# Loading ten tables at once and selecting from four of them unsplit, in a DLRM tower kernel

## The reference

```python
e = jnp.stack([tbl_f[ids[:, f]] for f in range(26)], axis=1)
combined = concatenate([dense[:, None, :], e], axis=1)            # 27 vectors a sample
interactions = einsum('bfd,bgd->bfg', combined, combined)
z = concatenate([dense, interactions[:, iu, ju]], axis=1)         # the 351 pairs
h = concatenate([z, dense], axis=1)
h = maximum(h @ W_top1 + b_top1, 0)                               # 607 -> 512
h = maximum(h @ W_top2 + b_top2, 0)                               # 512 -> 256
y = h @ W_top3                                                    # 256 -> 1
```

## Time and profile before

| | us |
|---|---|
| median of 3 runs | 474.64 |
| lowest and highest | 474.0, 475.17 |
| the profiled execution | 473.68 |
| its span in the profile | 471.9 |
| PE busy in the span | 409.8 (87%) |
| DVE busy | 298.0 (63%) |
| POOL busy | 250.7 (53%) |
| ACT busy | 240.6 (51%) |

### The profile page before, as it was taken

How to read it: one execution, slowest core, us unless ns; L and a number is a source line. 1 busy time by engine, 2 the same in 40 slices (tenths; PEclk the granted TensorE clock), 3 DMA queues, 4 the chain that set the end, 5 groups by cost and what they waited for, 6 DMA issues and landing times.

```text
span 471.9 us, 9190 instructions
## 1 busy us (share of the span) xinstructions
PE 409.8 (87%) x3384; PEld 383.0 (81%) x3384; DVE 298.0 (63%) x925; ACT 240.6 (51%) x558; POOL 250.7 (53%) x263
## 2 busy tenths in 40 slices
PE   1676799987998899998999799999999799888997
PEld 1565698876997799878898698988988699777876
DVE  3799597773556847665566766577665767544341
ACT  2341677562354745375454744466442834459462
POOL 0567355554555665656656556566666556564000
PEclk9979899998899999999999999999999999999999
DMA  7996134214132142223522153222522123111000
GB/s 192 255 264 170 39 72 100 67 35 100 46 71 64 41 102 66 64 57 59 97 63 74 39 81 79 73 64 51 96 72 71 44 71 77 41 43 32 13 1 0
DMA packets 24612, 35.95 MB, mean 76 GB/s; under 512 B 6296, under 2 KB 18720, under 8 KB 24568
## 3 DMA queue, kind: packets, MB, share of 16 engines
q1 hardware_dynamic: 16376, 18.57, 17.6%
q0 software_dynamic: 8192, 16.79, 14.2%
HBM read 35.33 MB, written 0.01 MB: 75 GB/s over the span
## 4 chain that ended last, share of the span: by engine, by line
PE 65%; DVE 9%; issue 7%; DMA 6%; ACT 6%; another core or an unknown queue 4%; SPq 1%; POOL 0%; POOLq 0%; DVEq 0%; ACTq 0%
PE gram_ps L425 18%; PE x_ps L406 14%; PE x_ps L407 12%; DVE hot L888 7%; PE x_ps L387 6%; DMA rows<-in_tbl_dram,ids_sb 5%; PE tail_ps L470 3%; PE tail_ps L468 3%; PE tail_ps L469 3%; ACT x L647 3%; PE tail_ps L460 2%; DVE gram L866 1%; DMA x<-in_tbl_dram 1%; ACT pairs L647 1%
## 5 line engine op out<-in xcount | busy, mean ns | idle before, releaser
L353 POOL DMA_INDIRECT rows<-in_tbl_dram,ids_sb x256 | 250.0, 976 | 186.9 <-PE x_ps L406 49.2
L888 DVE TENSOR_SCALAR hot<-ids_all,row_f 125x256 fp32r<-125x256 int32 x640 | 195.8, 374 | 53.8 <-PE x_ps L407 37.8
L406 PE MATMUL x_ps<-hot,table_hi 125*128 125x256 f32 x640 | 166.9, 297 | 36.4 <-issue 11.9
L406 PEld LDWEIGHTS x_ps<-hot,table_hi 125*128 125x128 f32 x640 | 124.3, 194 | 46.7 <-issue 35.5
L407 PE MATMUL x_ps<-hot,table_lo 125*128 125x256 f32 x640 | 160.5, 286 | 0.2
L407 PEld LDWEIGHTS x_ps<-hot,table_lo 125*128 125x128 f32 x640 | 124.7, 195 | 0.6 <-issue 0.6
L425 PE MATMUL gram_ps<-x 128*108 128x108 f32 x1024 | 109.8, 261 | 4.2 <-issue 3.2
L425 PEld LDWEIGHTS gram_ps<-x 128*108 128x108 f32 x1024 | 104.2, 177 | 5.7 <-issue 3.6
L647 ACT ACTIVATE picked<-x_ps 128x256 f32<-128x256 f32 x80 | 30.5, 382 | 90.4 <-PE x_ps L407 54.1
L866 DVE COPY gram<-gram_ps 44x208 f32<-44x208 f32 (+1 forms) x120 | 44.3, 369 | 32.3 <-remote 20.2
L647 ACT ACTIVATE gram<-gram_ps 44x208 f32<-44x208 f32 (+3 forms) x136 | 45.9, 337 | 32.3 <-remote 13.6
(11 more groups left out here) (74 smaller groups left out, 342.1 us busy)
## 6 DMA issues: line engine op xcount, KB each, us to landing
ids_all<-in_selected_ids_dram SPq DMA_DIRECT2D x80, 128.0 KB
rows<-in_tbl_dram,ids_sb POOLq DMA_INDIRECT x256
x<-in_tbl_dram SPq DMA_DIRECT2D x6, 448.0 KB
stage<-in_tbl_dram SPq DMA_DIRECT2D x3, 448.0 KB
rows<-in_r_dense_features_dram SPq DMA_DIRECT2D x16, 64.0 KB
stage<-in_W_pairs_dram SPq DMA_DIRECT2D x1, 702.0 KB
stage<-in_W_dense_dram SPq DMA_DIRECT2D x2, 256.0 KB
stage<-in_W_dram SPq DMA_DIRECT2D x1, 512.0 KB
```

The lines of the kernel that those rows point to most:

```text
L353: pool.indirect_dma_start(out=rows[t][:, slot, :], out_offset=None, in_=tables[GATHERED[slot - 1]], in_offset=bass.IndirectOffsetOnAxis(ap ...
L406: first = pe.matmul(bank, table_hi[j][:, c, :], v, start=(c == 0), stop=False)
L888: last = dve.tensor_scalar(hot[h][:, c, :], ids_all[0:VK, j % IDS, :], row, None, ALU.is_equal)
```

## The change

All ten raw tables get a home of their own, `raws`, in the very memory of the `table_lo` tensors; a table is split in place. SP loads all ten tables one after the other, with their ids; those of tables 5 to 9 go into new buffers `ids_start` in the memory of `x`. The weights come right behind, without a wait, and then the ids of macro tile 1. `loads_begun` is signalled after table 1.

Tables 2, 4, 6 and 8 (`WHOLE_TABLES`) are selected from as loaded at the start: eight float32 products in place of sixteen float32r ones (`select_whole`). ACT makes their high parts as before; DVE makes their low parts in macro tile 0, between the one-hots of tables 0 and 1 of the next macro tile.

The one-hots of the start go through five buffers in turn (`START_HOTS`), three of them in the memory of `x`; from macro tile 1 on they have two as before. The gathers begun are 24 and 23 in steps 0 and 1 in place of 22 and 22, so from step 1 on three more are ahead, and the first five have no ticks to wait for.

```diff
+    START_HOTS = 5
+    WHOLE_TABLES = [2, 4, 6, 8]
+    SPLIT_ORDER = [j for j in range(NS) if j not in WHOLE_TABLES] + WHOLE_TABLES
+    def hot_place(number):
+        return number % START_HOTS if number < 2 * NS else number % HOTS
-    BEGUN = [22, 22, 34, 34, 34, 34, 34, 34]
-    assert len(BEGUN) == NM and sum(BEGUN) + 8 == NM * GATHERS
+    BEGUN = [24, 23, 34, 34, 34, 34, 34, 34]
+
+    FREE = 4
+    assert len(BEGUN) == NM and sum(BEGUN) + 5 == NM * GATHERS
...
-                return ticks + number * ticks_of(step) // begun
+                free = FREE if step == 0 else 0
+                return ticks + max(number - free, 0) * ticks_of(step) // (begun - free)
...
-                sp.wait_ge(hi_ready, 6)
-                sp.wait_ge(lo_ready, 6)
                 sp.dma_start(w1a_raw, W1_dense[0:D, :]).then_inc(weights_loaded, 16)
...
-            for j in range(RAWS):
+            for j in range(NS):
                 if j < IDS:
                     load_ids_all(0, j)
+                else:
+                    load_ids_start(j)
                 load_table(j)
-            sp.sem_inc(loads_begun, 1)
+                if j == 1:
+                    sp.sem_inc(loads_begun, 1)
             for t in range(TILES):
                 load_dense(0, t)
             load_ids(TILES, B // P, ids_loaded[1])
-            for j in range(IDS, NS):
-                if IDS < j <= IDS + NS - RAWS:
-                    load_table(RAWS + j - IDS - 1)
-                sp.wait_ge(hot_ready, 2 * (j - IDS + 1))
-                load_ids_all(0, j)
             load_weights()
...
+            def select_whole(j):
+
+                pe.wait_ge(raw_loaded[j], 32)
+                bank = x_bank(0, start_use(j))[:].rearrange("p a b -> p (a b)")[:, 0:MACRO]
+                for c in range(VC):
+                    number = hot_number(0, j, c // HALF)
+                    if c % HALF == 0:
+                        pe.wait_ge(hot_ready, number + 1)
+                    last = pe.matmul(bank, table_raw[j][:, c, :], hot_buffers[hot_place(number)][:, c % HALF, :].bitcast(F32),
+                                     start=(c == 0), stop=(c == VC - 1))
+                    if c % 2 == 0:
+                        last.then_inc(paced, 1)
...
             def macro_tile(m, before):
                 transposes(m, 0, 2)
-                if not before:
-
-                    act.wait_ge(lo_ready, NS)
                 join(m, 1, 0)
...
+            def split_table(j):
+                dve.wait_ge(hi_ready, j + 1)
+                if j in WHOLE_TABLES:
+
+                    dve.wait_ge(x_filled, x_before(0, start_use(j) + 1))
+                low_part(table_lo[j][:], table_raw[j], table_hi[j][:]).then_inc(lo_ready, 1)
...
+                if not before:
+                    for j in WHOLE_TABLES:
+                        split_table(j)
                 build_hot(m + 1, 1)
...
             for j in range(1, NS):
-                split_table(j)
+                if j not in WHOLE_TABLES:
+                    split_table(j)
                 build_hot(0, j)
```

More of the change, by code:

```diff
@@ L94, in start_use, with hot_number, hot_ahead @@
         return j - EARLY - NS
+    START_HOTS = 5
+    WHOLE_TABLES = [2, 4, 6, 8]
+    SPLIT_ORDER = [j for j in range(NS) if j not in WHOLE_TABLES] + WHOLE_TABLES
+    def hot_number(m, j, h):
+        return m * 2 * NS + 2 * j + h
+    def hot_place(number):
+        return number % START_HOTS if number < 2 * NS else number % HOTS
+    def hot_ahead(number):
+        return max((n for n in range(number) if hot_place(n) == hot_place(number)), default=None)
     def x_end(m, t):
@@ L164, in dlrm_kernel @@
         rows = [sb(f"rows{t}", [P, 1 + NG, D]) for t in range(TILES)]
+        with nc.sbuf_tensor("hots_start", [P, MACRO * F], F32R) as hots_start:
+            pass
+        with nc.sbuf_tensor("ids_start", [P, NS - IDS, MACRO], I32) as ids_start:
+            pass
         x = sb("x", [D, MACRO, F])
@@ L179, in dlrm_kernel @@
         table_hi = [sb(f"table_hi{j}", [VK, VC, D], F32R) for j in range(NS)]
+        with nc.sbuf_tensor("raws", [VK, NS, VC, D], F32) as raws:
+            pass
         table_lo = [sb(f"table_lo{j}", [VK, VC, D], F32R) for j in range(NS)]
@@ L211, in dlrm_kernel @@
         weights_loaded = sem("weights_loaded")
-        raw_loaded = [sem(f"raw_loaded{i}") for i in range(RAWS)]
+        raw_loaded = [sem(f"raw_loaded{j}") for j in range(NS)]
         loads_begun = sem("loads_begun")
@@ L215, in dlrm_kernel @@
         lo_ready = sem("lo_ready")
+        ids_start_loaded = [sem(f"ids_start_loaded{j}") for j in range(NS - IDS)]
         ids_all_loaded = [sem(f"ids_all_loaded{i}") for i in range(IDS)]
@@ L246, in x_slots, with ids_of, wait_hot_read @@
             return x[:, t * P:(t + 1) * P, s0:s1]
+        def ids_of(m, j):
+            if m == 0 and j >= IDS:
+                return ids_start[0:VK, j - IDS, :], (ids_start_loaded[j - IDS], 16)
+            loads = 1 if m == 0 else 1 + (m - 1) * (NS // IDS) + j // IDS + 1
+            return ids_all[0:VK, j % IDS, :], (ids_all_loaded[j % IDS], 16 * loads)
         def tail_done(m, q):
             return (last_tail_filled, q + 1) if is_last(m) else (tail_filled, m * T_USES + (q + 1))
+        def wait_hot_read(eng, number):
+            m, j, h = number // (2 * NS), number // 2 % NS, number % 2
+            if h == 0:
+                eng.wait_ge(hot_read, m * NS + j + 1)
+            elif m == 0:
+                eng.wait_ge(x_filled, x_before(0, start_use(j) + 1))
+            else:
+                eng.wait_ge(x_filled, x_before(m - 1, x_use(m - 1, "table", j) + 1))
         def wait_tail_moved(eng, m, q):
@@ L315, in next_inputs @@
                 for j in range(IDS):
[L316 removed]
+                    wait_hots(m - 1, j if m == 1 else j + IDS)
                     load_ids_all(m, j)
@@ L607, in _ @@
             for j in range(NS):
-                select(-1, j)
+                if j in WHOLE_TABLES:
+                    select_whole(j)
+                else:
+                    select(-1, j)
             pe.wait_ge(ident_ready, 2)
```

76 lines of the change are left out of this document (34 added, 42 removed).

## The result

The changed kernel took 472.11 us in the median of 20 runs (467.37 to 478.27), the kernel before 474.51 in 20 runs on the same chip: a ratio of 0.994 with a 95% interval of 0.9914 to 0.9966. The ratio leaves out executions more than 1.5% above the fastest of their kernel, which the medians hold. So it is faster, but by 2.4 us where 12.1 were forecast, and the time lies above the range of 457 to 470. The profiled execution took 469.72 (span 467.9) against 473.68.

The account below looks back on a forecast made before the run. DVE was taken to bound the start and PE the macro tiles; -7.4 + 1.9 - 1.1 - 4.0 - 0.6 - 0.9 = -12.1 from 473.68 gave 461.6, as a median 462.5 us. Range 457 to 470.

Parts of the forecast that it names:

- The start: Start, before macro tile 0: four splits fewer and five one-hot buffers let DVE end at 39.1 instead of 46.55, -7.4 us.
- The margin of 0.8 us: Start: tables 7 and 9 with their high parts come 0.8 to 0.9 us before DVE wants them.
- the tables: Start: table 9 arrives at 33.5, gathers in front of it included, and delays DVE by 0 to 2 us, priced 0.
- Does a gather wait for what was issued earlier?: DMA queues: gathers and the ids of macro tile 1 wait for everything issued before them, so these ids come at 42.
- Late ids and splits, +1.9: Macro tile 0: late ids and 4.8 us of splits make PE's next half 1.7 us late, with next one-hots +1.9.
- with a stretch at half clock in it as well, 3.5: Macro tile 0: upper end of the price for late ids and splits, 3.5 us instead of the 1.9 taken.
- Gathers three earlier: From step 1 on, waits for gathers vanish: -1.1 at 91.85, -4.0 in macro tile 1, -0.6 at 231.13, -0.9 in the last tile.
- The neighbour argument: Macro tile 1: it lasts 58.3 us, the next 54.5, so its gain was taken as -4.0, near that neighbour.
- the first rival: Whole kernel: all waits are given back in full, no late ids, half clock recovered too, 455.4 us; chance 0.15.
- Macro tiles 2 to 6, -0.6: Steady macro tiles: only the wait of 1.06 us at 231.13 shrinks, -0.6 us (0 to 1.1).
- The start gains less: Rival: dearer gathers, half clock in a whole table or DVE behind in macro tile 0 lose 4 to 6 us; chance 0.20.
- The slow rival: Start: PE runs at half clock, selections end at 57.7 in place of 47.7, total 482.9 us; chance of slower 0.04.

Follow-up runs that it names:

- the later chips: Three chips of the follow-up runs, each with the kernel before beside them: it takes 440 to 442 us there, the changed kernel 431 to 433.
- the gathers begun late: Changed kernel with `loads_begun` signalled after table 6 as before, not after table 1: 432.04 us, 0.9804 of the kernel before.
- the third chip: Changed kernel run again unmodified, beside the kernel before at 440.23 us: 432.36 us, ratio 0.9813; again there: 430.95 us, 0.981.
- the second chip: Changed kernel run again unmodified, beside the kernel before at 442.05 us: 433.13 us, ratio 0.9812.
- the kernel with the ids first: Changed kernel with the ids of tables 0 to 2 for macro tile 1 loaded before the weights: 426.13 us, 0.9663; elsewhere 0.9667 and 0.9676.
- the gathers alone: Kernel before with only the gathers begun changed, 24 and 23 in place of 22 and 22: 429.11 us beside 441.28, ratio 0.9733.

## Why the prediction was wrong, step by step

The forecast was 12.1 us, and 2.4 were measured in the medians, 4.0 in the profiled pair. One term of the sum is shown to have failed, the price of the late ids and the splits. What the steady tiles lost on the first chip is the other half of the miss, and its cause stays open.

**The start: right on the first chip.** -7.4 was forecast and -7.55 measured in the profiled pair; DVE ended at 38.8 (39.1), the first transposes were at 39.89 (40), the first select at 44.43 (44.5). On the later chips it was worth less, 4.15 us (45.10 to 40.95). The kernel before is 2.6 us sooner there, so there was less to win: DVE's pause of 2.29 us at 23.23, which the prediction took for a wait for PE's reading, carries the releaser "remote", and on the later chips it is absent (on the second the same one-hots run from 19.43 to 22.07 without a break). So some 2.3 of the 7.4 us were that chip's and not the kernel's. The margin of 0.8 us that the prediction gave the tables is used up as well: DVE waits 0.2 to 0.5 us for the high part of table 9. Its step "the tables" held on the first chip (table 9 at 33.89, forecast 33.5); in the three later profiles of the changed kernel table 9 is there at 34.55 to 35.08, 1.1 to 1.6 us late.

**Does a gather wait for what was issued earlier?** The prediction took this from the earlier trace rows. With gathers begun at 4.87, the queues of the changed kernel on the first chip read, from 10 to 12 us:

```profile
q1 hardware_dynamic: 233, 0.43, 84.1%
q0 software_dynamic: 41, 0.09, 17.9%
```

Gathers move beside the table loads, a few microseconds after their own issue (none from 5 to 8 us, the first packets from 8 to 10). So the earlier trace rows did not show one common line in the order of issue. The Trainium skill (DMA: Bandwidth & Descriptors, section Queues, rings and completion order) says that each DMA engine goes round between the queues at every packet; this trace agrees in so far as both queues move in the same two microseconds, with 84% of the engines' time for one and 18% for the other. But the rule is not the whole of it: with the gathers begun late, from 13.73 on, none of their bytes moved before 26 us, as none had before 19 in the kernel before.

What the gathers took from the tables was low too. The prediction put "some ten" in front of table 9, 2.6 us; it came 3.5 us later than with late gathers. The queue of the gathers in the changed kernel on the third chip, from 4 us to table 9 at 34.7, has the reason:

```profile
q0 software_dynamic: 540, 1.11, 15.4%
```

1.11 MB are 17 gathers of 64 KB, against one in the same stretch of the other kernel, so the number was off and not the price of one (3.5 / 16 is 0.22 us, forecast 0.26). The ids for macro tile 1, on SP's own queue behind the weights, came late in every run that has them there, as the other half of the same step said.

**Late ids and splits, +1.9: this term failed.** The times in it were right: ids at 42.9 (42.0 forecast), the splits at 45.03 for 4.63 us, the second select at 51.00 (50.4). Its price was wrong. It was summed as one delay of PE of 1.7 us and 0.2 for the next one-hots, with nothing behind it. In the profiled pair macro tile 0 lost 6.5 us, on the second chip 5.5 (45.48 to 85.06 is 39.58, before 34.12), and the runs price the late ids at 5.5 to 6.7 in the total. Those runs are of the later chips; on the first one the kernel with the ids first was not run, so there the price rests on the profiled pair alone. The missing part is named in the prediction as an upper end ("with a stretch at half clock in it as well, 3.5"), and even that was low. In the four profiles of the changed kernel PE waits for one-hots one to three times in macro tile 0, 2.1 to 4.7 us in all (before: 0 to 0.6), and stands at half clock for 6.8 to 10.2 us of it (before: 0 to 3.4; the gathers alone: 6.8). With the ids ahead of the weights the waits fall to 0.9 us or less and the half clock to 0 or 3.4, and macro tile 0 is about as long as in the kernel before (34.8 to 35.9 beside 34.1 and 35.7). The whole then came to 0.966, 15 us better than before. That is more than the forecast gain, but not by the forecast's terms: 12.2 of it are the gathers, which had 6.6 in the sum, and 3.0 the start, which had 7.4.

**Gathers three earlier: right, and undersold.** -5.1 was forecast in macro tile 1, -5.5 measured in the pair and -9.3 on the second chip; no wait for rows is left there. The neighbour argument (no less than 54.5) did not hold: the tile took 52.9 on the first chip. On the others the full return of the first rival came true for this stage, including the half clock behind the wait: tile 1 is as long as its neighbours (48.4 and 48.5). Run alone, the gathers gave -12.2 us, where the terms for them in the sum come to -6.6.

**Macro tiles 2 to 6, -0.6: wrong in the first comparison.** +4.9 were measured, 4.5 of them as longer busy time of PE, with three half-clock stretches that before does not have. The sum took it that the clock there stays as it was, and gave no reason. On the second chip the changed kernel's steady tiles are as long as before's (48.5 to 48.8 against 48.6 to 49.7), so the change has not disturbed them. The theory that it did fell with that. What remains is an execution whose clock varies: of the 20 runs of the changed kernel the four with a mean clock of 0.982 took 467.4 to 470.1 us, the seven with 0.968 or less 472.2 to 478.3. The profiled execution of the kernel before has 0.982 as well and took 473.68, so by that one execution the change is worth 3.6 to 6.3 us there at the same mean clock. Why the clock varies more on that chip is open.

**The rivals.** "The start gains less" (467 to 468.5) names the right stage, macro tile 0 ("or DVE falls behind through macro tile 0"), and gave it 0.20. It deserved more: the prediction itself had put late ids in front of 4.8 us of splits on the one engine that the next select waits for. The slow rival with float32 products at half clock did not come: a whole table took 3.7 us at full clock on PE, forecast 3.4. Two halves of one, in the timeline after:

```profile
22.13 3.69 PE L441 MATMUL x_ps<-hots_start,raws 125*128 125x256 f32 x16 [0.17 <-issue]
```

## What to carry to other kernels

When loads are pulled forward, list what is pushed behind them on the same queue, and ask for each who waits for it and what work stands behind that wait: here 128 KB of ids behind 1.7 MB of weights, in front of 4.6 us of splits, took back the gain of a rebuilt start. Either of the two alone cost macro tile 0 nothing that shows, and a few lines of code parted them. Price a short pause of PE by the pauses that follow it and by the half-clock stretch that may come with it, not by its own length. And test the cheap part of a change by itself: two numbers in a list were worth more than all the rest.

## What the runs showed of the hardware

The same program takes 474 us in one comparison and 440 to 442 in four others on three chips, at nearly the same mean clock (0.982 and 0.984 in the profiled executions). Of the 6.2 us by which the steady tile shown above differs, 4.1 are idle time of PE between its instructions. A forecast from one chip's trace carries that chip's idle time into every term.

The clock is not decided by the program alone. The kernel with the ids first has the same pause of PE before its second transposes in three profiled executions (1.24, 1.26 and 1.25 us); behind it PE is at half clock from 44.6 to 48.1 in the second, and in the other two it keeps the full clock there.

The first two gathers begun at 13.73, beside the table loads, took POOL 8.02 and 5.03 us, where the first two begun at 4.87 took 0.95 to 1.10. But full DMA engines alone do not explain it: in the kernel before the first one, at 13.15 and beside table loads too, took 1.10. Why these differ was not tried.

```profile
13.73 8.02 POOL L395 DMA_INDIRECT rows<-in_tbl_dram,ids_sb  x1 [12.15 <-SPq L349]
22.05 5.03 POOL L395 DMA_INDIRECT rows<-in_tbl_dram,ids_sb  x1 [0.30 <-issue]
```
